# Attention with routed experts in one program: PSUM banks dealt out anew, side work moved ahead of the weighted values, expert tiles spread over the steps

## The reference, cut to what matters

```python
xn = layernorm(x)                       # x: 4 batches, 1024 rows, 128 columns
Q, K, V = heads(xn @ Wq.T), heads(xn @ Wk.T), heads(xn @ Wv.T)   # 16 heads of 8 columns; Q, K turned by rope
attn = softmax(Q @ K.T / sqrt(8))       # per batch and head 1024 x 1024
a = merge(attn @ V) @ Wo.T
w, idx = top_k(xn @ Wg, 2)              # 2 of 8 experts per row
out_e = relu((xhat * gamma_e + beta_e) @ W1_e + b1_e) @ W2_e + b2_e + xn    # W1: 128 x 512, W2: 512 x 128
y = x + a + sum over the 2 experts of softmax(w) * out_e
```

## Time and profile before

| | us |
|---|---|
| median of 3 runs | 631.59 (631.28 to 632.95) |
| the profiled execution | 634.26 |
| its span | 632.4 |
| PE busy | 602.0 (95%) |
| ACT busy | 506.0 (80%) |
| DVE busy | 380.2 (60%) |
| POOL busy | 217.5 (34%) |

### The profile page before, as it was taken

How to read it: one execution, slowest core, us unless ns; L and a number is a source line. 1 busy time by engine, 2 the same in 40 slices (tenths; PEclk the granted TensorE clock), 3 DMA queues, 4 the chain that set the end, 5 groups by cost and what they waited for, 6 DMA issues and landing times.

```text
span 632.4 us, 12274 instructions
## 1 busy us (share of the span) xinstructions
PE 602.0 (95%) x4620; PEld 254.1 (40%) x4620; DVE 380.2 (60%) x1108; ACT 506.0 (80%) x552; POOL 217.5 (34%) x267
## 2 busy tenths in 40 slices
PE   8889989998999999999999999999999999999894
PEld 7324312223454544334445454433344545444121
DVE  4846588888556555567554655468556555543572
ACT  2678899897777878888878787888887878888992
POOL 4299700017754343222333433322223334311000
PEclk9989999999999999999999999999999999999996
DMA  6156501002110202001120110200102021110720
GB/s 239 28 153 197 160 1 35 1 7 58 51 31 26 64 26 60 16 16 29 40 56 18 42 51 26 55 18 14 51 19 59 18 63 28 24 43 14 295 76 35
DMA packets 25362, 35.48 MB, mean 56 GB/s; under 512 B 5440, under 2 KB 15728, under 8 KB 24784
## 3 DMA queue, kind: packets, MB, share of 16 engines
q1 hardware_dynamic: 19936, 23.70, 12.4%
q0 software_dynamic: 4544, 9.32, 5.6%
q10 hardware_dynamic: 816, 1.61, 0.7%
HBM read 17.36 MB, written 8.85 MB: 41 GB/s over the span
## 4 chain that ended last, share of the span: by engine, by line
PE 75%; ACT 13%; DVE 5%; issue 2%; SPq 2%; DMA 1%; DVEq 1%; ACTq 0%; POOL 0%
PE acc L644 29%; ACT ring L857 13%; PE sc L610 13%; PE bank L699 12%; PE bank L689 11%; PE bank L681 3%; PE bank L538 2%; SPq L322 2%; PE bank L709 2%; DVE xn L1217 1%; DMA wr<-L_attn_W_k 1%; PE sc L538 1%; PE sc L496 1%; PE bank L513 1%; DVE blocks L1027 1%
## 5 line engine op out<-in xcount | busy, mean ns | idle before, releaser
L857 ACT ACTIVATE ring<-sc 128x1024 f32<-128x1024 f32 x512 | 492.9, 1022 | 99.1 <-PE sc L610 98.0
L644 PE MATMUL acc<-ring,v 128*9 128x512 f32 x2048 | 269.4, 598 | 2.4 <-issue 2.4
L610 PE MATMUL sc<-qs,ks 32*128 32x512 f16 x1024 | 135.5, 385 | 12.3 <-ACT ring L857 8.3
L483 POOL DMA_INDIRECT token_out<-work,token x71 | 75.6, 1065 | 185.8 <-DVE work L1237 179.1
L473 POOL DMA_INDIRECT work<-normed,token x71 | 71.3, 1004 | 160.3 <-DVE work L1223 95.1
L1230 DVE TENSOR_SCALAR work<-bank,xn 128x128 f32<-128x128 f32 x284 | 79.8, 344 | 42.2 <-PE bank L689 42.2
L699 PEld LDWEIGHTS bank<-xn,work 128*128 128x128 f32 x568 | 70.7, 191 | 62.5 <-issue 35.0
L699 PE MATMUL bank<-xn,work 128*128 128x128 f32 x568 | 86.2, 287 | 1.4 <-DVE work L1223 1.4
L689 PE MATMUL bank<-work,xn 128*128 128x128 f32 x568 | 82.8, 282 | 2.1 <-DVE norms L922 1.4
L689 PEld LDWEIGHTS bank<-work,xn 128*128 128x128 f32 x568 | 73.9, 197 | 26.8 <-issue 25.0
L610 PEld LDWEIGHTS sc<-qs,ks 32*128 32x128 f16 x1024 | 36.6, 91 | 104.3 <-ACT ring L857 71.2
(11 more groups left out here) (177 smaller groups left out, 331.3 us busy)
## 6 DMA issues: line engine op xcount, KB each, us to landing
w_all<-L_ffn_W SPq DMA_DIRECT2D x16, 256.0 KB, 5.0
qs<-hl SPq DMA_DIRECT2D x60, 64.0 KB
ks<-hl SPq DMA_DIRECT2D x60, 64.0 KB
x<-L_attn_x SPq DMA_DIRECT2D x4, 512.0 KB, 7.8
normed<-xn SPq DMA_DIRECT2D x4, 512.0 KB, 3.7
xn<-token_out SPq DMA_DIRECT2D x2, 1024.0 KB, 5.8
w_all<-token_out SPq DMA_DIRECT2D x2, 1024.0 KB, 11.3
out<-x SPq DMA_DIRECT2D x8, 256.0 KB, 2.2
```

The source lines that it names most:

```text
L483: pool.indirect_dma_start(out=y_d[:, :], in_=ys[done % TILE_BUFFERS], in_offset=None, out_offset=bass.IndirectOffsetOnAxis(ap=token[:, 1, ...
L610: last = nc.tensor.matmul(dst, ks[r:r + 32, kb * P:(kb + 1) * P], qs[r:r + 32, at], start=True, stop=not slow)
L644: last = nc.tensor.matmul(acc[qh % 2][32 * j:32 * j + VW, :], v9[:, b, kb, 4 * g + j, :], ring[:, (2 * n + j // 2) % UNITS, j % 2, :], sta ...
L857: nc.scalar.activation(ring[:, (2 * n + u) % UNITS, :, :], sc[u][:, :].rearrange("p (h c) -> p h c", h=2), ACT.Exp, scale=SCALE / (1 << SC ...
```

## The change

- `sc` becomes three pairs of banks; unit k = 2n + u uses pair k % 2 for the first four units and (k - 2) % 3 after. PE waits once per step, for the exponential of unit 2n, before both units of step n + 1.
- `acc` becomes one bank. `weigh` in the first step of a group of eight waits for the `tail` of the group just ended.
- One bank (`aside_bank`, index 0) serves all pieces of the loop. The transposed columns of tile t + 1 are made inside `layer_two(t)` and taken by DVE right after `rows_out(t)`.
- PE runs `aside(n)` ahead of `weigh(n)`.
- At most one piece per step; expert tiles are always two pieces, spread evenly over steps 53 to 235. `place` moves from step 24 to 23, `gates` from 23 to 26, the columns of b1, gamma and beta (`COLUMNS_AT`) from step 5 to 25, `ranks` from 21 to 22, `tokens` from 48 to 47; values come in 3 pieces per batch in place of 4, `invert` in 8 pieces with the sum over groups taken on DVE (`take_named`).
- `turned` has four tiles in place of two.

```diff
-WO_AT, COLUMNS_AT = 3, 5
-TURN_AT = {6: (1, 0), 7: (1, 1), 9: (2, 0), 11: (2, 1), 13: (3, 0), 15: (3, 1)}
+WO_AT, COLUMNS_AT = 3, 25
+MOMENTS_AT = {1: 2, 2: 3}
+VALUE_TILES = ((0, 3), (3, 6), (6, 8))
+TURN_AT = {6 + 5 * k + h: (1 + k, h) for k in range(B - 1) for h in range(2)}
+VALUES_AT = {8 + 5 * k + m: (1 + k, m) for k in range(B - 1) for m in range(len(VALUE_TILES))}
+TOP_AT = {4: 0, 11: 1, 16: 2, 20: 3}
-ROUTE_AT, RANKS_AT, PLACE_AT, SLOTS_AT = 20, 21, 23, 24
+ROUTE_AT, RANKS_AT, SLOTS_AT, GATES_AT = 21, 22, 23, 26
...
+FFN_FROM, FFN_TO = 53, 237
+TAKEN = [n for at in (PLAIN_AT, NORM_AT, FLAG_AT, PROJECT_AT) for n in at]
+FIRST, SECOND = {}, {}
+for n in range(FFN_FROM, FFN_TO):
+    used = len(FIRST) + len(SECOND)
+    due = (n + 1 - FFN_FROM) * 2 * SLOT_TILES
+    if n not in TAKEN and used * (FFN_TO - FFN_FROM) < due:
+        (SECOND if used % 2 else FIRST)[n] = used // 2
...
+def score_pair(k):
+
+    return k % 2 if k < 4 else (k - 2) % 3
...
-        sc = [ctx.enter_context(nc.psum_tensor(f"sc{k}", [P, 2 * CH], F32)) for k in range(2)]
-        acc = [ctx.enter_context(nc.psum_tensor(f"acc{k}", [P, CH], F32)) for k in range(2)]
-        bank = [ctx.enter_context(nc.psum_tensor(f"bank{k}", [P, CH], F32)) for k in range(2)]
+        sc = [ctx.enter_context(nc.psum_tensor(f"sc{k}", [P, 2 * CH], F32)) for k in range(3)]
+        acc = ctx.enter_context(nc.psum_tensor("acc", [P, CH], F32))
+        aside_bank = ctx.enter_context(nc.psum_tensor("aside_bank", [P, CH], F32))
+        second_acc, bank = sc[2][:, 0:CH], [aside_bank[:, :], sc[2][:, CH:2 * CH]]
...
                 if kb == 0:
-                    wait(pe, acc_out, qh - 1)
+                    wait(pe, acc_out, qh)
...
+            def layer_two(t):
+                pe.wait_ge(bank_taken[0], USE["one", t])
+                enter_bank(0, "two", t)
+                if t + 1 < SLOT_TILES:
+                    turn_tile(t + 1)
+                for c in range(FC):
+                    last = nc.tensor.matmul(bank[0][:, 0:D], hT[t % 2][:, c, :],
                                             w_tile[t % 3][:, W2_AT + c * D:W2_AT + (c + 1) * D],
                                             start=(c == 0), stop=(c == FC - 1))
...
+                    if n + 1 == 2:
+                        pe.wait_ge(bank_taken[1], USE["rotated", 0])
+                    if n + 1 >= 2:
+                        pe.wait_ge(e_ok, 2 * n + 1)
                     for u in range(2):
-                        wait(pe, e_ok, 2 * n + u + 1)
+                        if n + 1 == 1:
+                            pe.wait_ge(e_ok, u + 1)
                         scores(n + 1, u, slow)
...
+                        aside(n)
                         weigh(n)
-                        aside(n)
```

More of the change, by code:

```diff
@@ L133, in bank_uses @@
     for n in range(STEPS):
[L134 to L165, removed]
+        pieces = [(name, *(at[n] if isinstance(at[n], tuple) else (at[n],))) for name, at in (
+            ("turn", TURN_AT), ("values", VALUES_AT), ("invert", INVERT_AT), ("plain", PLAIN_AT), ("norm", NORM_AT),
+            ("bound", FLAG_AT), ("out", PROJECT_AT), ("one", FIRST), ("two", SECOND)) if n in at]
+        pieces += [(name,) for name, at in (("wo", WO_AT), ("rows", COLUMNS_AT), ("ranks", RANKS_AT),
+                                            ("tile", FFN_FROM - 1)) if n == at]
+        assert len(pieces) <= 1
+        for piece in pieces:
+            take(0, *piece)
     take(0, "out", B - 1, 1)
@@ L655, in turn_rows @@
                 pe.wait_ge(rows_in, 48)
-                enter_bank(1, "rows")
-                nc.tensor.transpose(bank[1][:, 0:48], rows[0:48, :], ident[0:48, 0:48]).then_inc(bank_full[1], 1)
+                enter_bank(0, "rows")
+                nc.tensor.transpose(bank[0][:, 0:48], rows[0:48, :], ident[0:48, 0:48]).then_inc(bank_full[0], 1)
             def ranks():
                 pe.wait_ge(pick_ok, 1)
-                enter_bank(1, "ranks")
-                nc.tensor.matmul(bank[1][:, 0:T * E], before, cnt[:, 0, :, :], start=True, stop=True)
@@ L663, in ranks @@
-                nc.tensor.matmul(bank[1][:, T * E:2 * T * E], ones[:, :], cnt[:, 0, :, :], start=True, stop=True
-                                 ).then_inc(bank_full[1], 1)
-            def invert(g, part):
-                if part == 0:
-                    pe.wait_ge(mark_ok, g + 1)
-                if (g, part) == (0, 0):
-                    enter_bank(1, "tokens")
-                for i in range(GROUP // 2 * part, GROUP // 2 * (part + 1)):
-                    last = nc.tensor.matmul(bank[1][:, 0:2 * SLOT_TILES], place_mark[g % 2][:, i, :],
+                enter_bank(0, "ranks")
@@ new lines, in ranks, with invert @@
+                nc.tensor.matmul(bank[0][:, 0:T * E], before, cnt[:, 0, :, :], start=True, stop=True)
+                nc.tensor.matmul(bank[0][:, T * E:2 * T * E], ones[:, :], cnt[:, 0, :, :], start=True, stop=True
+                                 ).then_inc(bank_full[0], 1)
+            def invert(g):
+                pe.wait_ge(mark_ok, g + 1)
+                enter_bank(0, "invert", g)
+                for i in range(GROUP):
+                    last = nc.tensor.matmul(bank[0][:, 0:2 * SLOT_TILES], place_mark[g % 2][:, i, :],
@@ L679, in tile_in @@
                 pe.wait_ge(xt_in[t % TILE_BUFFERS], 16 * (t // TILE_BUFFERS + 1))
[L680 to L688 removed]
+                return nc.tensor.transpose(bank[0][:, D:D + P], xt[t % TILE_BUFFERS], ident)
@@ L694, in layer_two @@
-            def layer_two(t, c0, c1):
-                if c0 == 0:
-                    pe.wait_ge(bank_taken[0], USE["one", t])
-                    enter_bank(1, "two", t)
-                for c in range(c0, c1):
-                    last = nc.tensor.matmul(bank[1][:, 0:D], hT[t % 2][:, c, :],
+                last.then_inc(bank_full[0], 1)
+            def layer_two(t):
[3 more added lines that the diff above has]
+                    turn_tile(t + 1)
+                for c in range(FC):
+                    last = nc.tensor.matmul(bank[0][:, 0:D], hT[t % 2][:, c, :],
```

272 lines of the change are left out of this document (129 added, 143 removed).

## The result

The changed kernel takes 635.06 us (median of 11 runs, 633.78 to 635.98) where the kernel before, on the same chips, takes 632.48 us (11 runs, 631.28 to 634.07). The ratio is 1.0039, with a 95% interval of 1.0027 to 1.0052: slower by 0.4%. I had forecast 629.0 us and a gain of 0.4%.

The account below looks back on a forecast made before the run. PE was taken to bound the long stage, two thirds of the span, and ACT the end. Stage terms +1.9 - 0.3 - 1.3 - 1.4 - 1.25 = -2.4 us, from 631.6, gave 629 us; the range was 616 to 640.

Parts of the forecast that it names:

- Steps 6 to 25: Early stage, 48.88 us before: step 5 stall removed, but PE waits behind `place` for the transpose of `tail(2)`; +1.9 us.
- I take 1.5 us for the first weighted values: After PE's pause for the transpose of `tail(2)`: the first weighted values run slow, 1.5 us.
- Steps 26 to 49: Stage of 48.97 us before: `mark` and `invert` hide, PE waits behind `tokens` for the transpose of `tail(5)`; -0.3 us.
- Steps 50 to 61: Stage of 31.53 us before: PE waits for DVE about 2 us at tile 0 and 1 us at the norm; -1.3 us.
- Steps 62 to 235: Long stage, 416.24 us before: PE's need of 395.3 plus 19.5 us of new waits gives 414.8; -1.4 us.
- PE's need of 395.3: Long stage: PE's own sum in us for scores, values, tiles, `plain`, output projections, norms and flags.
- the two plain sections: Long stage, around each `plain`: `take_plain`, `split` and relu share DVE's queue, and one bank holds back first layers; 13.2 us.
- term (b): Long stage, `tail` with one `acc`: the transpose must fit between two `weigh`; 6.3 us in all.
- Steps 236 on: End: step 236 shorter without a transpose, output projection of step 252 covered by the extra pair, no `merge` stall; -1.25 us.
- the first: Rival, no change: what the pair gives is eaten in full, long stage at 416, whole 630.6 us; chance 0.18.
- the third: Rival, slower: layers followed by `weigh` cost PE 0.06 us more in some 170 steps, +10, 639 us; chance 0.24.
- The second: Rival: the waits are hidden, 6 of the 19.5 us remain, or `place` holds PE less; 616 us; chance 0.22.

Follow-up runs that it names:

- experiment 3: The kernel before with one edit, the columns of b1, gamma and beta taken in step 25 in place of 5: 629.39 us, ratio 0.9956.
- experiment 1: The changed kernel with `place` one step later (24 in place of 23), behind the transpose of `tail(2)`: 628.79 us, ratio 0.9943.
- experiment 6: The changed kernel with no piece of the experts in the steps that hold a `split`: 625.89 us, ratio 0.9897.
- experiment 2: The changed kernel with `place` one step later (24) and `tokens` one step later as well (48): 628.53 us, ratio 0.9932.
- experiment 4: The changed kernel with the third score pair taken away, everything else of the change kept: 664.26 us, ratio 1.0502.
- experiment 9: The changed kernel with `place` and the marks (all but the first) later, `tokens` in step 49, no piece in steps of a `split`: 614.03 us, ratio 0.9696.
- experiment 8: The kernel of experiment 2 with the marks two steps later (all but the first) and `tokens` in step 49: 626.65 us, ratio 0.9913.
- experiment 11: The changed kernel with the weighted values ahead of the piece in each step, as before the change: 695.25 us, ratio 1.0969.

## Why the prediction was wrong

The direction was wrong, by 5 us out of 630; the places were right, and the time was in the range. Step by step:

- **Steps 6 to 25, +1.9; measured +3.76.** Removing the stall of step 5 is worth 3.8 us by itself (experiment 3). Held against e(6), PE came back from the hole 1.1 us later than I had it (50.2 us after e(6), not 49.1): 0.3 us had gone before the last piece of values left PE, and the chain of DVE behind it took 18.6 us in place of 17.8. And from there to the next exponential it took 2.48 us (values 1.90, scores 0.61 at the lower clock), where I charged 1.7. That term, "I take 1.5 us for the first weighted values", was sized from a shorter pause of the earlier trace rows.
- **Steps 26 to 49, -0.3; measured +0.81.** The same term again: 2.47 us from PE's return to the exponential in place of 1.8, and 0.4 for the wait itself. `mark` and `invert` did hide, because PE had stood for ten microseconds while DVE worked off `place`; in experiment 1 they no longer did. The cover was the other hole, and the prediction did not see that.
- **Steps 50 to 61, -1.3; measured -0.73.** Right in sign.
- **Steps 62 to 235, -1.4; measured +1.23.** PE's need of 395.3 held to the prices. Of the 19.5 us of waits 13.2 were put on the two plain sections, where 12.2 were found, and experiment 6 shows that they are collisions with `split` and the bank: 9.5 of them go with one line. Outside the two sections I had 6.3, and the measured length leaves 10.0. All 6.3 were put on the tails, term (b), and the relu was put at nothing ("fits as before"). That is the step that failed. The trace names 7.9 of the 10.0 us: transposes 2.9 (1.30 of it behind the empty step 144, as forecast, but 0.54 where I had 1.5 behind 232), relu 2.9, ACT 1.6, `rows_out` 0.5. So the single accumulator cost less than half of its term, and waits that the sum left out cost 5.0. Of the relu's 2.9 us 1.56 are the one late relu of step 225, which DVE began 1.6 us after its first layer had ended; experiments 1 and 2, with the same schedule, don't have it and take 414.6 and 414.5 us, as I had forecast (414.8). So this stage's miss of 2.6 us is about the size of what sets two traces of one schedule apart. What made that relu late, and where the other 2.1 of the 10.0 us went, stays open.
- **Steps 236 on, -1.25; measured -1.43.** Right.

Of the rivals, the first (the pair is eaten in full, long stage near 416) comes nearest as a difference to the kernel before (-1.0 us where +2.6 was measured; the third had +7.4), and its long stage is near what was measured. The outcome, slower, had been the third's. But the first one's mechanism is false: experiment 4 shows that the pair gives 17 us there. The rule of the Trainium skill beside it (TensorE: Matmul & The Clock Gate, HAM oscillation), by which double buffering in PSUM gave that kernel nothing further, does not carry to this one: here a third pair is worth 29 us in all. The second (waits hidden, 616) is what experiment 9 reaches, 614, when they are moved apart by hand. The third (the new order costs PE) is false in its mechanism: the tile's pitch is 4.85 us as in the earlier trace rows, and the old order is 60 us slower in this kernel.

So the change is a trade that comes out near zero: with two pairs in both, the new dealing of banks and work costs 18 us of the long stage, and the third pair gives 17 back. The hole before step 24 eats what the early stage gains. My forecast had all of this in it and summed small differences of large terms; each miss was under 3 us, and those of the four stages from step 6 to 235 all lay on the side of a loss.

## What to carry to other kernels

When a bank is taken from one use for another, look for every place where the engine that empties the remaining bank has a long block in its queue: with one buffer, the order of DVE's queue is PE's order. Four such places (`place`, the marks, `tokens` and the splits), each moved by a few numbers in a table of steps, were together worth 21 us in a change that had been 2.6 us slower. A stall that is removed also uncovers what its idle time had hidden, so move the blocks together and measure them together.

## What the runs showed of the hardware

- After PE had waited 9.84 us and again after 3.00 us, the next weighted values took 1.90 and 1.89 us in place of 1.05 and the scores 0.61 in place of 0.40, at a granted clock of 0.50, the lower of the two levels; after 9.84 us the group behind was slow as well. Such a wait so cost another 1.1 us behind it. The length of the wait alone does not tell whether the clock falls: after 1.90 us in step 22 of experiment 2 the values took 1.82 us, after 2.44 us in step 32 of experiment 8 they took 1.05.
- A busy share can fall from 95% to 89% in a kernel of nearly the same time: matmuls of one engine are drawn overlapping, and pauses of about 0.25 us between them, as in the kernel before, are counted as busy.
- Traces of one schedule differed by 3 to 5 us in a stage of 410 us (414.5 and 417.4; 409.2, 408.4 and 404.4), and half or more of that were one or two relus that DVE began 1.6 to 2.0 us late. Whole runs of one kernel spread over 2.2 us (the change) to 9.4 us (experiment 11). A stage's difference of 1 to 2 us in single traces is no finding by itself.
